# Cross-attention on one core: the turned mask blocks stand ahead of the context products in TensorE's queue

## What is computed

```python
Q = _split_heads(query @ Wq.T + bq, B, LQ)
K = _split_heads(key @ Wk.T + bk, B, LK)
V = _split_heads(value @ Wv.T + bv, B, LK)
scores = jnp.einsum('bhqd,bhkd->bhqk', Q, K) / np.sqrt(HD)
scores = jnp.where(mask[:, None, :, :] == 0, jnp.float32(-1000000000.0), scores)
attn = jax.nn.softmax(scores, axis=-1)
ctx = jnp.einsum('bhqk,bhkd->bhqd', attn, V)
ctx = ctx.transpose(0, 2, 1, 3).reshape(B, LQ, H)
out = ctx @ Wo.T + bo
x = out + query
```

## Time and profile before

| | us |
|---|---|
| median of 3 runs | 1685.32 |
| lowest and highest | 1681.8, 1688.21 |
| the profiled execution's own time | 1685.78 |
| its span, from the first to the last instruction | 1683.8 |
| PE busy | 1611.8 (96%) |
| PEld busy | 1031.3 (61%) |
| POOL busy | 1409.5 (84%) |
| ACT busy | 1353.2 (80%) |
| DVE busy | 1168.6 (69%) |
| mean granted TensorE clock | 0.98 |

### The profile page before, as it was taken

The page is one execution under the profiler, slowest core; times in us unless marked ns, Lnnn a source line. Parts: engine busy times, 40 slices in busy tenths (PEclk is TensorE's granted clock), DMA queues, the critical chain, the costliest instruction groups (busy, mean ns, idle before and its releaser), DMA issues.

```text
span 1683.8 us, 25426 instructions
## 1 busy us (share of the span) xinstructions
PE 1611.8 (96%) x7997; PEld 1031.3 (61%) x7997; DVE 1168.6 (69%) x2852; ACT 1353.2 (80%) x1559; POOL 1409.5 (84%) x883
## 2 busy tenths in 40 slices
PE   7879999999999999999999999999999999999986
PEld 5545666666666666666666666666666666666633
DVE  6557776767777677776767677776777767677734
ACT  3667888897988889788888878888797978878773
POOL 5566889898898989889898989989888998988694
PEclk9989999999999999999999999999999999999977
DMA  7867576775867777577676668677676867757401
GB/s 250 262 186 229 146 230 188 218 217 158 240 186 217 199 199 221 164 236 191 208 218 182 219 173 239 185 209 212 173 235 165 240 177 213 223 166 228 102 9 69
DMA packets 180196, 327.54 MB, mean 195 GB/s; under 512 B 37344, under 2 KB 37344, under 8 KB 180064
## 3 DMA queue, kind: packets, MB, share of 16 engines
q1 hardware_dynamic: 180064, 325.93, 66.5%
HBM read 236.72 MB, written 89.13 MB: 194 GB/s over the span
## 4 chain that ended last, share of the span: by engine, by line
PE 77%; DMA 11%; DVE 6%; POOL 3%; ACT 1%; issue 1%; SPq 0%; DVEq 0%; POOLq 0%; ACTq 0%
PE proj_bank L1078 37%; PE ring L961 12%; PE exp_banks L976 12%; PE ctx_bank L992 11%; DMA stack_scratch<-qk_lo 10%; DVE qk_lo L813 2%; DVE ring L772 2%; PE ring L1012 2%; PE ring L1021 1%; DVE qk_hi L810 1%; PE ctx_bank L1078 1%; ACT qk_hi L658 1%; POOL total L494 1%; DMA b_all<-ln_b_dram 1%; POOL c_lo L472 0%
## 5 line engine op out<-in xcount | busy, mean ns | idle before, releaser
L772 DVE CUSTOM_DVE_ANT_0 ring<-ring,bias 128x512 f32<-128x512 f32 x1024 | 689.9, 710 | 306.7 <-PE ring L961 305.2
L638 ACT ACTIVATE probs<-exp_banks 128x1024 f32<-128x1024 f32 x512 | 524.4, 1024 | 230.2 <-PE exp_banks L976 227.9
L609 ACT CAST exp_banks<-biasT 128x1024 f32<-128x1024 bf16 x512 | 520.8, 1017 | 23.1
L961 PE MATMUL ring<-k_stack,q_stack 96*128 96x512 f32 x1024 | 334.7, 404 | 20.2 <-DVE maxes L772 17.2
L976 PE MATMUL exp_banks<-q_stack,k_stack 98*128 98x512 f32 x1024 | 327.5, 402 | 2.6 <-ACT exp_banks L609 2.6
L502 POOL TENSOR_TENSOR total<-total,probs 128x1024 f32<-128x1024 f32 x126 | 299.3, 2398 | 9.1
L494 POOL TENSOR_TENSOR total<-total,probs 128x2048 f32<-128x2048 f32 x63 | 290.5, 4610 | 9.9 <-ACT probs L638 1.5
L494 POOL TENSOR_TENSOR total<-probs 128x2048 f32<-128x2048 f32 x63 | 289.7, 4598 | 0.0
L992 PE MATMUL ctx_bank<-probs,v 128*32 128x512 f32 x2048 | 278.6, 616 | 0.7 <-DVE recipT L839 0.7
L961 PEld LDWEIGHTS ring<-k_stack,q_stack 96*128 96x128 f32 x1024 | 194.9, 190 | 82.8 <-DVE maxes L772 35.3
L976 PEld LDWEIGHTS exp_banks<-q_stack,k_stack 98*128 98x128 f32 x1024 | 194.4, 191 | 56.8 <-issue 10.1
(11 more groups left out here) (131 smaller groups left out, 2239.6 us busy)
## 6 DMA issues: line engine op xcount, KB each, us to landing
w_tile<-w_scratch SPq DMA_DIRECT2D x120, 512.0 KB, 3.7
k_stack<-stack_scratch SPq DMA_DIRECT2D x192, 256.0 KB, 4.6
q_stack<-stack_scratch SPq DMA_DIRECT2D x192, 256.0 KB, 6.7
stack_scratch<-qk_hi SPq DMA_DIRECT2D x128, 256.0 KB, 2.7
stack_scratch<-qk_lo SPq DMA_DIRECT2D x128, 256.0 KB, 3.7
c_raw<-cT_dram SPq DMA_DIRECT2D x64, 256.0 KB, 3.9
x_raw<-xT_dram SPq DMA_DIRECT2D x64, 256.0 KB, 4.5
mask_raw<-mask_dram SPq DMA_DIRECT2D x64, 256.0 KB, 5.7
```

Of the source, the lines that this page charges most:

```text
L609: nc.scalar.copy(exp_banks[:, 2 - 2 * wave:4 - 2 * wave, :], biasT[:, kc:kc + 1, :].to_broadcast([P, 2, L])).then_inc(seeded, 1)
L638: nc.scalar.activation(probs[:, u % PS, 2 - 2 * wave:4 - 2 * wave, :], exp_banks[:, 2 - 2 * wave:4 - 2 * wave, :], ACT.Exp).then_inc(exps, 1)
L772: nc.vector.tensor_tensor_reduce(out=ring[:, n % 2], in0=ring[:, n % 2], in1=bias[:, c], scale=1.0, scalar=LOWEST, op0=ALU.subtract, op1=A ...
L961: nc.tensor.matmul(ring[:, n % 2], q_stack[0:3 * D, at, c * P:(c + 1) * P], k_stack[0:3 * D, at, :], start=True, stop=True).then_inc(ring_ ...
```

## The change

Two statements of PE's step change places. The mask block is issued ahead of the context products of the same step instead of behind them. The ring numbers, all waits and the other engines' code stay as they are.

```diff
                 shifted_scores(y, 1)
                 score(y, 2)
                 score(y, 3)
+                if PLAN.mask(y):
+                    turn_mask(*PLAN.mask(y)[1:])
                 if 0 <= y - 1 < UNITS:
                     context(y - 1)
-                if PLAN.mask(y):
-                    turn_mask(*PLAN.mask(y)[1:])
                 if PLAN.sums(y) and PLAN.sums(y)[1] < LAST:
                     sum_probs(PLAN.sums(y)[1])
```

## The result

| | before | after |
|---|---|---|
| median, us | 1686.76 | 1733.68 |
| lowest and highest, us | 1681.8, 1688.93 | 1730.32, 1735.38 |
| runs | 4 | 4 |
| span of the profiled execution, us | 1683.8 | 1733.4 |

The changed kernel is slower by a ratio of 1.0277, with a 95% interval from 1.0256 to 1.0298. The forecast was 1730.1 us and a ratio of 1.027.

What follows compares the result with a forecast made beforehand. PE was taken to bound the kernel; 60 blocks x 0.86 = 51.6 us, less 6.8 taken up, added 44.8 us to the profiled 1685.78, giving 1730.6, or 1730.1 us for the median; range 1720 to 1739.

Steps and rivals of the forecast that it cites:

- The bound: Regular part, 140 to 1590 us: PE sets the pace; a step 14 takes 6.01 us with PE busy throughout.
- The moved wait: Mask block ahead of the context products: PE stands 0.77 us until DVE has read score 2, read ending at +0.95.
- The size of the term: Each mask step grows by 0.86 us (bounds 0.72 and 0.96), 0.77 of it the stand, the rest change of width.
- the restart: Before the mask block: from the end of DVE's read to PE's next weight load, 0.06 us.
- What took it up: Steps 13, where the projection already waits for line 813, take up 6.8 us of the added time.
- The block of y = 1: First sequence: PE's later 9.29 us stand takes up the loss, 0 us; uncovered it would be 0.9.
- The waits for line 813 in the other steps: Steps 9 and 10: their chains begin at an earlier PE product and move with PE, so nothing is taken up.
- the first rival: Later stands in steps 9, 10 and 13 shrink too, taking up at most 21.5 us: 1715 us; chance 0.05.
- The sum: Whole run: 60 blocks x 0.86 = 51.6, less 6.8, gives 44.8 us added.
- the granted clock did not fall: Clock rival: more stands bring PE to 1.2 GHz, one mask step per sequence adding 77 us: 1807; chance 0.02.
- DVE did not set the pace: Rival: DVE paces the mask steps, PE's stand is free, 7.0 us of copy waits return: 1678; chance 0.02.
- the bank was not free in time: Rival: score 2's bank is free when PE reaches the mask block, wait not felt, time unchanged; chance 0.01.

Runs made afterwards that it cites:

- the larger dose: Against the changed kernel, the mask block also waits until DVE has read score 3; 1791.52 us, ratio 1.0628 to the kernel before.

## Why the prediction was right

**The bound.** PE set the pace in the regular part, as read. The steps 14 took the whole of what was added (0.92 us each, 0.71 of it idle time of PE), and the run with steps 14 alone shows that nothing later gives it back.

**The moved wait.** This was the step that carried the sum, and it held: DVE's read still ends at +0.95, PE stands until then, 60 times. The two sides were shown apart. The wait in the old order costs 0.68 us a step, the new order without the wait 0.06; the rest of the 0.92 comes only with both, and the rows above place it.

**The size of the term.** It was 0.86 us and measured 0.92. The part at fault is the restart. I took 0.06 us from the end of the read to the next load, from a place where a score waits for one semaphore. Here the block's first load goes out at 784.79, 0.12 us behind the read's end at 784.67, and its first product 0.03 later. In the run with the wait alone the context products' first load went out after 0.05. In the trace the mask block's wait for the bank is carried by an instruction of PE's sequencer of its own, 0.05 us long, and the load goes out behind it. The number of semaphores alone does not make the difference: the context products of that run wait for two as well, but there the load itself carries the wait that ends last. No run exchanged the two waits of the block, so it is read from the trace and not tested that this instruction makes the 0.07 us. From the load to the context products it took 785.13 - 784.79 = 0.34 us (0.35 taken), and from there to the projection's load 0.99 (1.00 taken), +2.40 in all where +2.36 was forecast. The last 0.02 us are at the projection's first product, which lasts 0.50 us instead of 0.47.

A score is followed by a full-width product after 0.23 us and by the context products after 0.32; behind the block it is 0.33 us to the context products (0.31 in the changed kernel), where the projection followed after 0.21. By TensorEngine Tiling, Key Properties, of the Trainium skill a change of tiling mode drains the array. The trace agrees with that, though no run separates a drain from another cost of the narrow products.

**What took it up.** The steps 13 took up 15 x 0.92 - (103.90 - 97.11) = 7.0 us, with 6.8 forecast. The block of y = 1 added nothing that lasted: its step grew by 0.9 us and the next two shrank by as much. The waits for line 813 in the other steps stayed: the steps 9 and 10 had 13.7 us of them before and 13.0 after, and the steps 13, which had 3.1, have none. So the first rival fell. Of the 64 blocks that the prediction speaks of, 61 changed places, since those of y = -3 to -1 have no context products in their step; its sum counts only 60 and is not touched by this.

**The sum.** 60 x 0.92 less 7.0 is 48.2 us, against 44.8 forecast and 46.9 between the medians. The forecast was 3.4 us short in this sum, 60 times the 0.06 us of the term. The spans of the two profiles differ by 49.6, with the steps 9 and 10 and the start adding chance.

**The other rivals.** In the first profile of the changed kernel the granted clock did not fall. Its stretch from 140 to 1640 us (length, busy time, then the clock):

```profile
140.00:1640.00 1500.00, 1444.73 (x7261) 932.96 (x7260) 1041.43 (x2587) 1222.68 (x1410) 1275.13 (x778) 1.00 0.67 194
```

In its second profile the clock fell once, behind a stand of 1.90 us in a step 9 (below). The prediction called a clock under 1.00 between 140 and 1590 us a sign of being wrong. It is no such sign: the kernel before does the same in its second profile, and no fall of the changed kernel follows one of the new stands.

DVE did not set the pace, and the bank was not free in time; 42.3 us of stands say so. The 7.0 us that DVE no longer waits for the block bought nothing.

## To carry to other kernels

Before an instruction is moved ahead in an in-order queue, look at when its wait is met in the old place, not only at its own cost: these four products of 0.2 us had 0.37 us of slack behind 1.0 us of other work, and in front of that work they held it all up. What a stand costs depends on what stood behind it already, so count each kind of step by itself. Where a block has two places, the better one here was behind independent work that covers the release it needs; moving the producer up instead can only help if its own wait is met there, and here it cost 6 us.

## What the runs showed beyond that

In single steps 9 the clock did fall. The second profile of the kernel before has such a stand, and PE's clock in stretches of 2 us around it:

```profile
1135.46 1.22 PE L1078 MATMUL proj_bank<-c_hi,w_tile 128*128 128x512 f32 x2 [1.91 <-DVE qk_lo L813]
```

```profile
1132.00:1134.00 2.00, 1.55 (x11) 0.28 (x9) 0.13 (x1) 1.97 (x3) 1.92 (x4) 1.00 1.06 409
1134.00:1136.00 2.00, 0.54 (x1) 0.50 (x2) 1.96 (x5) 1.97 (x4) 0.85 (x3) 0.84 0.53 203
1136.00:1138.00 2.00, 2.00 (x6) 1.56 (x5) 0.93 (x5) 0.22 (x1) 1.13 (x3) 0.50 0.49 183
```

After PE had been idle for 1.91 us the granted clock went from 1.00 to 0.50, that is from 2.4 to 1.2 GHz, and the step lasted 8.84 us where its neighbours take 6.2 to 7.0. The second profile of the changed kernel has the same behind a stand of 1.90 us in a step 9:

```profile
856.00:858.00 2.00, 0.87 (x4) 0.74 (x5) 1.96 (x5) 1.86 (x3) 0.53 (x3) 1.00 0.71 276
858.00:860.00 2.00, 2.00 (x7) 1.56 (x6) 0.75 (x4) 0.58 (x1) 1.46 (x3) 0.62 0.37 126
```

The length of the stand alone does not tell whether the clock falls. A stand of 1.84 us in the first profile of before left it at 1.00, while one of 1.65 us in a step 9 of the run with score 2 early and the block behind was followed by 0.50. In the run with the larger dose ten stands of 1.88 to 2.52 us in steps 13 left the clock at 1.00, and five of 1.90 to 2.64 us were followed by the lower level. The prediction had counted stands of this length as harmless, and that was luck of one profile; for the new ones of 0.7 us it held in both profiles, as it did for 45 stands of 1.27 us in the larger dose. In the two kernels compared it is the stand of step 9 that puts the clock at risk, with the change and without it; a longer wait in the mask steps brings the steps 13 to it as well.
